# Routed experts: Pool's adds of full tiles behind the next W1 part, y gated later with two gate buffers

## The reference, cut to what matters

```python
x = x * rsqrt(mean(x * x) + eps) * ln_w          # xn
vals, idx = top_k(xn @ Wg + bg, 2)
topk_w = softmax(vals)
for e in range(8):                                # per expert, D = 256, F = 1024
    a = xf @ W1a[e] + b1a[e]
    b = xf @ W1b[e] + b1b[e]
    y = silu(a) * b @ W2[e] + b2[e]
    acc = acc + w_e[:, None] * y
out = x + gb * acc                                # gb: gate of the token's batch element
```

## Time and profile before

| | us |
|---|---|
| median of 3 runs | 2402.96 (2402.96 to 2404.33) |
| the profiled execution | 2401.95 |
| its span | 2400.2 |
| routed experts, from the first up matmul | 1684.8 to 2400.2 |
| PE busy | 2201.6 (92% of the span) |
| DVE busy | 1734.0 (72%) |
| ACT busy | 1309.6 (55%) |
| POOL busy | 948.9 (40%) |

### The profile page before, as it was taken

One profiled execution on the slowest core, in us unless ns is written; L12 is line 12 of the kernel. 1 busy time (PEld: TensorE's weight loads), 2 busy tenths in 40 slices (PEclk: granted clock), 3 DMA queues, 4 the chain that ended last, 5 costly groups with the idle time before them and its releaser, 6 DMA issues. The chain is left out here.

```text
span 2400.2 us, 39193 instructions
## 1 busy us (share of the span) xinstructions
PE 2201.6 (92%) x12976; PEld 1401.9 (58%) x12976; DVE 1734.0 (72%) x2837; ACT 1309.6 (55%) x2549; POOL 948.9 (40%) x1084
## 2 busy tenths in 40 slices
PE   7978999999999999988999689982999999999998
PEld 5852333333333333326777556652788888888887
DVE  7768787878788787825777768864666767666765
ACT  5533777677677777773233244431555555555554
POOL 4652330313121220213555422445355545555555
PEclk9987999999999999998999899985999999999999
DMA  5669035436161711004000100112554545454542
GB/s 202 165 159 120 2 82 107 87 85 116 56 124 53 138 73 39 8 1 137 1 0 0 34 9 18 54 60 92 173 146 136 145 134 160 126 164 124 169 123 51
DMA packets 126583, 220.29 MB, mean 92 GB/s; under 512 B 16448, under 2 KB 92608, under 8 KB 126016
## 3 DMA queue, kind: packets, MB, share of 16 engines
q1 hardware_dynamic: 104368, 173.28, 21.3%
q0 software_dynamic: 22032, 44.64, 13.6%
HBM read 138.83 MB, written 78.67 MB: 91 GB/s over the span
## 5 line engine op out<-in xcount | busy, mean ns | idle before, releaser
L232 DVE TENSOR_REDUCE tile_max<-p_m 128x2 f32<-128x1024 f32 (+1 forms) x628 | 641.8, 1064 | 134.9 <-PE p_m L224 67.5
L1021 ACT ACTIVATE probs<-p_s 128x512 f32<-128x512 f32 (+3 forms) x1280 | 596.2, 534 | 240.0 <-PE p_s L924 234.7
L2300 PE MATMUL p_up<-f_xT,f_w 128*128 128x512 f32 (+1 forms) x2304 | 474.0, 355 | 24.5 <-POOL f_w L2526 12.7
L2300 PEld LDWEIGHTS p_up<-f_xT,f_w 128*128 128x128 f32 x2304 | 370.0, 189 | 85.7 <-issue 26.2
L864 POOL TENSOR_SCALAR_AFFINE_SELECT probs<-probs 128x128 f32<-128x128 f32 x512 | 145.0, 292 | 695.4 <-ACT probs L1021 686.5
L221 PE MATMUL p_m<-ka,qa 96*128 96x512 bf16 (+1 forms) x1256 | 352.5, 363 | 12.8 <-DVE tile_max L232 5.0
L924 PE MATMUL p_s<-qa,ka 99*128 99x512 bf16 (+3 forms) x1280 | 351.7, 351 | 13.3 <-ACT probs L1021 7.1
L2526 POOL TENSOR_TENSOR f_w<-f_raw,f_w 128x1024 fp32r<-128x1024 f32 x95 | 230.9, 2437 | 276.7 <-ACT f_w L2355 276.7
L938 PE MATMUL p_o<-probs,va 128*32 128x512 f32 (+3 forms) x2560 | 300.3, 541 | 0.8 <-issue 0.5
L2315 PE MATMUL p_y<-f_w,f_hidden 128*128 128x256 f32 x1872 | 252.6, 281 | 0.9 <-DVE f_hidden L2453 0.5
L221 PEld LDWEIGHTS p_m<-ka,qa 96*128 96x128 bf16 x1256 | 108.3, 99 | 237.9 <-DVE tile_max L232 135.8
(11 more groups left out here) (279 smaller groups left out, 2724.2 us busy)
## 6 DMA issues: line engine op xcount, KB each, us to landing
x_slots<-mods SPq DMA_DIRECT2D x73, 518.0 KB, 4.2
f_raw<-in_W SPq DMA_DIRECT2D x24, 1024.0 KB, 11.3
f_raw<-in_W1a SPq DMA_DIRECT2D x23, 1024.0 KB, 6.6
f_raw<-in_W1b SPq DMA_DIRECT2D x23, 1024.0 KB, 9.0
qk_scr<-parts SPq DMA_DIRECT2D x48, 256.0 KB, 2.8
qa<-qk_scr POOLq DMA_DIRECT2D x42, 256.0 KB, 15.5
ka<-qk_scr POOLq DMA_DIRECT2D x42, 256.0 KB, 17.3
f_x<-x_slots SPq DMA_DIRECT2D x15, 518.0 KB, 3.8
```

The source lines that it names most:

```text
L232: return nc.vector.tensor_reduce(out=k.tile_max[:, 2 * hp:2 * hp + 2, i, bank], in_=products[:, :, 0:width], op=ALU.max, axis=AX.X)
L1021: nc.scalar.activation(probs[:, (buf * UNITS + n) % NPROBS, h, lo:CH], p_s[:, s_bank(("exp", HG * n + h), buf), lo:CH], ACT.Exp, scale=DH ...
L2300: last = nc.tensor.matmul(p_up[:, f % 2, ab, 0:size], w1[:, wh, ab * KT + kt, f * P:(f + 1) * P], xT[:, t % 2, xh, kt, 0:size], start=(kt, ...
```

## The change

Four things are moved, all in the routed experts. Pool: where tile t - 1 is a half tile, the adds of tile t - 2 (a full one) are issued behind the first W1 part of tile t, and no longer at the end of tile t - 1's list. This is so at t = 3, 6, 8, 11, 14, 16, 19 and 22. VectorE: `weigh_y` goes from block 2 to block 4, `weigh` from 4 to 5, `gate_of_y` from 5 to 7; the last tile keeps blocks 2 and 4 for `weigh_y` and `gate_of_y`. y_gate gets a second buffer, and ScalarE's wait for y_ready before it is for the tile two before. In the last tile y is biased and weighed by 128 rows, and each DMA of Pool waits for its own rows.

```diff
-        y_gate = m.sb("f_y_gate", [P, SPT, D])
+        y_gate = m.sb("f_y_gate", [P, 2, SPT, D])
...
-        WEIGH_Y_AT, HALF_GATE_AT, WEIGHTS_AT, GATE_AT = 2, 4, 4, 5
+        WEIGH_Y_AT, HALF_GATE_AT, WEIGHTS_AT, GATE_AT = 4, 4, 5, 7
+        LAST_WEIGH_Y_AT, LAST_GATE_AT = 2, 4
...
                     act.wait_ge(weights_ready, t + 1)
-                    if t:
-                        act.wait_ge(y_ready, t)
+                    if t >= 2:
+                        act.wait_ge(y_ready, t - 1)
                     for u in range(SIZES[t] // P):
-                        nc.scalar.activation(y_gate[:, u, :], k.mods[1][:, 0, GB, :], ACT.Copy,
+                        nc.scalar.activation(y_gate[:, t % 2, u, :], k.mods[1][:, 0, GB, :], ACT.Copy,
                                              scale=batch_weight[:, t % 2, 0, u:u + 1]).then_inc(half_gated, 1)
...
-                    if f == WEIGH_Y_AT and t:
+                    if f == (LAST_WEIGH_Y_AT if last_tile(t) else WEIGH_Y_AT) and t:
                         weigh_y(t - 1)
...
+                def last_y(t):
+
+                    dve.wait_ge(gate_ready_y, t + 1)
+                    dve.wait_ge(down_psum, FB * t + FB)
+                    dve.wait_ge(y_stored, 16 * blocks_to[t - 1])
+                    for u in range(SIZES[t] // P):
+                        row = y[:, t % 2, u, :]
+                        nc.vector.tensor_tensor(row, p_y[:, u, :], b2[:, t % 2, :], ALU.add).then_inc(last_biased, 1)
+                        dve.wait_ge(last_biased, u + 1)
+                        nc.vector.tensor_tensor(row, row, y_gate[:, t % 2, u, :], ALU.mult).then_inc(last_ready, 1)
...
-                        if f == GATE_AT:
+                        if f == (LAST_GATE_AT if last_tile(t) else GATE_AT):
                             gate_of_y(t)
...
-                take_y(NTILES - 1)
-                weigh_y(NTILES - 1)
+                last_y(NTILES - 1)
...
                 def scatter(t):
                     pool.wait_ge(y_to_ready, t + 1)
-                    pool.wait_ge(y_ready, t + 1)
+                    if not last_tile(t):
+                        pool.wait_ge(y_ready, t + 1)
...
+                        if last_tile(t):
+                            pool.wait_ge(last_ready, u + 1)
...
                                                     ALU.subtract).then_inc(w1_ready, 1)
+                        if q == 0 and t >= 2 and SIZES[t - 1] == HT:
+                            scatter(t - 2)
                     if not last_tile(t):
                         gap_exponential(t + 1)
-                    if t:
+                    if t and (SIZES[t] == ST or last_tile(t)):
                         scatter(t - 1)
```

8 lines of the change are left out of this document (5 added, 3 removed).

## The result

The changed kernel takes 2462.57 us (median of 4 runs, 2460.73 to 2467.74); the kernel before, run beside it, 2403.22. The ratio is 1.0250, 95% interval 1.0232 to 1.0267: slower by 59 us. The forecast was 2439, range 2418 to 2456. The direction came out and so did the size of the largest term by itself; the sum did not: it is 23 us short. The profiled execution of the changed kernel was the longest of its four, 2467.74 us, so its rows hold 65.8 us more than those of before.

What follows compares the result with a forecast made beforehand. TensorE was taken to bound full tiles; only half tiles lost time, some 2.5 us each, waiting for Pool and VectorE. Terms 27.2 + 7.2 + 1.9 - 0.5 = +36 gave 2438 us profiled, 2439 as median, range 2418 to 2456.

Steps and rivals of the forecast that it cites:

- Pool's order: At 8 seams from half into full tiles, four DMAs delay the second W1 part: +3.4 us each, +27 in all.
- TensorE has nothing else in its queue there: At the seam's block 2, matmuls behind it are issued in order, so nothing fills the +3.4 us stall.
- the later parts: W1 parts 3 and 4: due 8.4 and 16.8 us after part 2, ready 2.4 and 4.9 after it, hence hidden.
- The gate of y: VectorE's gate in block 7: half tile's first f_gate +2.0 us, shrinking to +0.9 a seam, +7 over 8 seams.
- Weigh beside Pool's subtraction: Behind block 5, a small operation takes 2.14 us, holds TensorE to E + 0.6, under block 2's E + 10.6: no cost.
- weigh_y two blocks later: Behind two full tiles, 6 places: first W1 part +1.2 us late at half tile's head, counted as nothing, bound 7.
- End and second buffer: Last tile's late first f_gate +1.9 us, y going out by block -0.5; second gate buffer 0.
- (a): Pool's freedom pays: VectorE's half-tile waits go, 8 seams each give back 2.5 us, 2383 us; chance 0.08.
- (b): VectorE's waits go, Pool's order stays: half tile gains 2.5 a seam, block 2 costs 3.4, 2410 us; chance 0.07.
- (c): The 3.4 us stall at each seam lowers TensorE's clock: 2.0 x 8 = +16, 2455 us; chance 0.15.

Runs made afterwards that it cites:

- pool_only: The kernel before with Pool's new order of the adds and nothing else changed: 2430.10 us, ratio 1.0107 to the kernel before.
- adds_end: The changed kernel with the moved adds behind all W1 parts of the next full tile, four row-number buffers: 2443.91 us, 1.0177 of the kernel before.
- adds_end_weigh4: adds_end with weigh alone back in block 4, where weigh_y also stands: 2435.51 us, ratio 1.0139 to the kernel before.

## Why the prediction was wrong

**Pool's order, +27: right in size by itself, in part by luck.** pool_only gives 26. In the changed kernel E, the end of the first W1 part's subtraction, is at 1943.71, and block 2 begins at 1953.48 = E + 9.77 (E + 10.6 forecast, E + 7.2 in the earlier trace rows). The gap to the first DMA is 0.17 us (0.6 was taken), the four DMAs take 7.15 (7.40), and the next subtraction starts 0.53 us before the last DMA's row ends and not 0.1 behind it, but takes 2.9 us and not 2.4. That is 0.8 us a seam less than forecast, and the clock, which the rival had priced apart, made up for it. With VectorE's new places in, Pool's order adds 17 us (adds_end against the changed kernel), which the forecast's plain sum did not allow for.

**"TensorE has nothing else in its queue there": wrong once VectorE's places move too.** The parts 2 and 3 that pile up behind the adds run in one piece, and while they do, VectorE's f_hidden of block 0 is held 5.41 us and f_y comes 1.19 us too late for the down matmuls. The text called the later parts hidden, since each was ready before TensorE needed it. It asked only for the parts themselves and not for what their subtractions do to VectorE. By itself Pool's order does not cost this wait: in pool_only the f_hidden of block 0 begins at E + 5.39, before the next subtraction at E + 6.95, and in the changed kernel at E + 7.20, behind it (E + 6.79).

**The gate of y, +2.0 us at the head, shrinking to +0.9, in all +7: the step that failed first.** The duration was right (3.86 us for four) and the head even worse, +2.64. The seam's end was near: E comes 23.89 us into the half tile and not 22.75, +1.14. But the step asked only for what the next seam gets of it. At the head itself the late f_gate of block 0 makes that of block 1 late, behind which take_y stands, and the down matmuls of block 0 wait for f_y: 1.75 us in each half tile, a wait that exists nowhere in the trace of before. Views: VectorE's and TensorE's timelines of the kernel before, half tile 7.

```profile
1904.08 1.21 DVE L2464 TENSOR_TENSOR f_y<-p_y,f_b 128x1024 f32<-128x1024 f32 x1
```

```profile
1905.44 0.94 PE L2315 MATMUL p_y<-f_w,f_hidden 128*128 128x256 f32 x6
```

There f_y ended at 1904.08 + 1.21 = 1905.29 and its down matmuls began at 1905.44: the reserve was 0.15 us, and the forecast had not looked. Measured for the whole term: 16 us with the adds out of the way, 20 to 22 with them in, where 7 was forecast.

**Weigh beside Pool's subtraction, TensorE at E + 0.6, "under E + 10.6 for block 2 and so costs nothing": wrong, and by its logic.** The duration was forecast (2.14, measured 2.35), and so was the hour: TensorE's block 0 began at 1944.54 = E + 0.83. But a wait at block 0 and one at block 2 don't cover one another by being under the same limit: TensorE pays 2.22 us at the first, of which 1.59 stood there before. And the late f_gate keeps the next operations of VectorE late as well, which is how f_hidden of block 0 gets behind the backlog above. With the adds at the end it measures 9 us (adds_end to adds_end_weigh4).

**weigh_y two blocks later, counted as nothing, bound 7: wrong.** The wait came as worked out, 1.22 us where 1.2 was forecast, six times, 7.3 us. The cover named for it, VectorE's chain at the half tile's end, doesn't cover: the late start makes that chain later too. Beyond this the later adds push the first W1 part's subtraction onto VectorE's W2 subtraction at the end of the full tile (4.65 us at 1854.40, where it took 1.23 before), and the f_gate behind it is late in turn. With the adds at the end it measures 17 us, more than the bound. In the changed kernel the two weighings were undone only together, for 12 to 14 us.

**End and second buffer, +1.4 and 0.** The +1.4 was +1.9 for the late first f_gate of the last tile and -0.5 for the by-row end. The first came: the last tile takes 30.23 us, 27.85 before, +2.4, and belongs to the gate's cost. The second is 0.3 us in the profile and can't be told in the time.

**The rivals.** (a) and (b) are out: the waits for VectorE grew. (c), the clock, came in a weaker form: about 11 us instead of 16, in six short stretches; pool_only has four, adds_end two. By the Trainium skill (TensorE: Matmul & The Clock Gate, HAM oscillation — how this bites in real kernels) waits of some 3 to 5 us between bursts of about 2 us bring the slow clock back each time. Here the matmuls between two waits fill far more than 2 us, and shorter waits were enough: single waits of 1.6 us never did it, waits of 2.2 us did at 1883.65 and did not at 1944.54, and one of the six stretches (2028.4) came behind a pair of 1.47 and 1.75 us close together. Whether a wait of 2.2 us lowers the clock or not I can't say from these runs.

The sum by what was measured: 26 for Pool's order, then 34 for VectorE's places (20 to 22 for the gate, 12 to 14 for the weighings), 0 for the end: 60, for a measured 59. It must come out, since the parts are differences between kernels that end at the changed one; what it shows is the division. The forecast had 27, 7, 0 and 1.4, so the gate and the weighings were 27 us short together and the other terms 2 to 3 too high. The result lies above the range for the same reason: the upper bound let VectorE's terms be at most 16 and 7, less what overlaps, and put weigh at nothing.

## What to carry to other kernels

Where an operation is moved in front of others on its engine, look up for each one behind it who waits for it and with what reserve, at its own place and not only at the end of the stage; a wait that the trace does not show may have a reserve of 0.15 us. A delay counted as hidden behind a later one must lie in parallel with it: two waits of the same in-order engine one after the other add up. And a burst of Pool's work that is ready in time for its own reader can still cost what VectorE doesn't get done while it lasts.
